# Two-layer Flamingo block on one core: logits pieces in banks of their own, gate selections behind the first pairs, first and last expert in halves of 256 rows

## What is computed

```
logits = xt @ wg                       # 2048 x 8
top two experts of each token, softmax weights of the two, renormalised
cap = 512 slots of each expert; a token's slot is its rank among those that chose the expert
y[slot] = gelu(x[slot] @ w1[e]) @ w2[e]; out[token] += gate * y[slot]
```

## Time and profile before

| | us |
|---|---|
| median of 3 runs (lowest, highest) | 574.84 (572.47, 578.08) |
| the profiled execution | 574.42 |
| its span in the trace | 572.7 |
| PE busy | 511.3 (89%) |
| DVE busy | 423.4 (74%) |
| ACT busy | 249.9 (44%) |
| POOL busy | 147.5 (26%) |

### The profile page before, as it was taken

How to read it: one execution, slowest core, us unless ns; L and a number is a source line. 1 busy time by engine, 2 the same in 40 slices (tenths; PEclk the granted TensorE clock), 3 DMA queues, 4 the chain that set the end, 5 groups by cost and what they waited for, 6 DMA issues and landing times.

```text
span 572.7 us, 8595 instructions
## 1 busy us (share of the span) xinstructions
PE 511.3 (89%) x3273; PEld 418.0 (73%) x3273; DVE 423.4 (74%) x794; ACT 249.9 (44%) x362; POOL 147.5 (26%) x120
## 2 busy tenths in 40 slices
PE   7887989897979899989999882899999999999990
PEld 3555667786969777767787651488999989999990
DVE  3799889999999885977977969564766848667340
ACT  1233566757675454526554511053534344343200
POOL 2053400000000021202212200720437355283144
PEclk9988999998989999979999995899999999999996
DMA  5511110000000010122221331211537475462031
GB/s 185 174 37 38 37 38 0 1 1 0 1 1 2 1 37 1 48 71 69 74 74 38 129 100 31 73 38 42 122 120 163 104 172 106 140 152 59 5 38 19
DMA packets 35118, 36.40 MB, mean 64 GB/s; under 512 B 3936, under 2 KB 33925, under 8 KB 34949
## 3 DMA queue, kind: packets, MB, share of 16 engines
q1 hardware_dynamic: 28933, 28.19, 15.5%
q0 software_dynamic: 6144, 7.66, 8.0%
HBM read 28.19 MB, written 8.39 MB: 64 GB/s over the span
## 4 chain that ended last, share of the span: by engine, by line
PE 58%; DVE 28%; issue 7%; ACT 3%; POOL 1%; DMA 1%; DVEq 0%; POOLq 0%; ACTq 0%
PE PS L1288 13%; PE PS L1289 13%; PE PS L1290 13%; PE PS L1619 4%; PE PS L1303 4%; PE PS L1498 3%; PE PS L1561 3%; DVE tmp L949 2%; DVE st L785 2%; DVE tmp L960 2%; PE PS L1628 2%; DVE xT_lo L809 2%; DVE hT_lo L968 2%; DVE xn L801 2%; DVE tmp L937 1%
## 5 line engine op out<-in xcount | busy, mean ns | idle before, releaser
L1288 PE MATMUL PS<-w_hi,hT_hi 128*128 128x256 f32 x384 | 110.5, 288 | 2.0 <-DVE hT_lo L968 2.0
L1290 PE MATMUL PS<-w_hi,hT_lo 128*128 128x256 f32 x384 | 109.4, 285 | 0.0
L1289 PE MATMUL PS<-w_lo,hT_hi 128*128 128x256 f32 x384 | 109.4, 285 | 0.0
L757 ACT ACTIVATE tmp<-PS,biasT 128x512 f32<-128x512 f32 x64 | 40.5, 685 | 103.9 <-PE PS L1290 103.8
L568 POOL DMA_INDIRECT out<-tmp,dst_idx x32 | 55.9, 1747 | 104.5 <-DVE tmp L1247 97.2
L1288 PE MATMUL PS<-xT_hi,w_hi 128*128 128x512 f32 (+1 forms) x200 | 79.4, 397 | 1.6 <-DVE tmp L837 1.1
L1289 PE MATMUL PS<-xT_lo,w_hi 128*128 128x512 f32 (+1 forms) x200 | 78.3, 392 | 0.0
L1290 PE MATMUL PS<-xT_hi,w_lo 128*128 128x512 f32 (+1 forms) x200 | 78.1, 391 | 0.0
L1288 PEld LDWEIGHTS PS<-w_hi,hT_hi 128*128 128x128 f32 x384 | 74.5, 194 | 3.8 <-DVE hT_lo L968 2.3
L1289 PEld LDWEIGHTS PS<-w_lo,hT_hi 128*128 128x128 f32 x384 | 74.4, 194 | 1.3
L1290 PEld LDWEIGHTS PS<-w_hi,hT_lo 128*128 128x128 f32 x384 | 74.2, 193 | 0.0
(11 more groups left out here) (211 smaller groups left out, 953.1 us busy)
## 6 DMA issues: line engine op xcount, KB each, us to landing
w_raw<-in_L_ffn_w SPq DMA_DIRECT2D x72, 256.0 KB, 3.3
residual<-in_x SPq DMA_DIRECT2D x4, 512.0 KB, 5.9
out<-residual SPq DMA_DIRECT2D x3, 512.0 KB, 4.7
normed_rows<-xn SPq DMA_DIRECT2D x3, 512.0 KB, 2.9
kv<-in_L_ffn_b SPq DMA_DIRECT2D x1, 1024.0 KB, 4.7
tmp<-in_L_xattn_Wq SPq DMA_DIRECT2D x2, 256.0 KB
out<-residual SPq DMA_DIRECT2D x2, 256.0 KB, 2.1
normed_rows<-xn SPq DMA_DIRECT2D x2, 256.0 KB, 3.1
```

Of the source, the lines that this page charges most:

```text
L757: act.activation(gD[:, G % 2, f, :], H[:, G % 2, f, :], ACT.Gelu, bias=biasT[:, col:col + 1]).then_inc(e_gelu, 1)
L1288: pe.matmul(o, lh, rh, start=start, stop=False, skip_group_check=skip)
L1289: pe.matmul(o, lh, rl, start=False, stop=False, skip_group_check=skip)
L1290: return pe.matmul(o, ll, rh, start=False, stop=stop, skip_group_check=skip)
```

## The change

1. **Piece 2** (tiles 8 to 11) is applied at t = 15 instead of 14 and turned at t = 16 instead of 15. Its logits columns and rows come after the loop instead of at t = 16, and `top_two(2)` stands after the last `x_lo`.
2. **Pieces 3 and 4** are transposed into PSUM banks of the scores (2 and 3), their logits go to banks 4 and 7. PE then waits for `c_shift`, `lgT_copied` or `lg_copied` in place of `T_free`. Before the last transpose stand 8 warming matmuls, and 5 after it (before: 3, 10 and 5). POOL's `power` of piece 3 comes before the last `low_parts` of that stage.
3. **Ranks:** three matmuls accumulate in one bank, and the DVE addition L1148 falls away. The tile-number selection goes from DVE (2 instructions) to ACT (16 small ones). The 32 instructions for `onehotB` become 4 on 1024 elements each. The small matmuls go by tile in four groups, each with a wait for ACT and one for DVE.
4. **Gate selections** are made at steps 2, 3 and 4 of the expert loop, `gates_of_slots` at step 5 (before: ahead of the loop, and at step 1), with the sums in bank 7.
5. **Experts 0 and 7** are done in two blocks of 256 rows: 40 steps instead of 32, of which 16 have `hidden` of 12 matmuls of 128x256 and `project` of 12. The first gather is of two tiles, and so is the second. Of the last expert, tiles 0 and 1 leave with the first block; tile 2 at `half_done`, and tile 3 from a bank of its own at the end.

```
-APPLY_AT, TURN_AT, COLUMNS_AT = {7: 0, 11: 1, 14: 2}, {8: 0, 12: 1, 15: 2, 16: 3}, {9: 0, 13: 1, 16: 2, 17: 3}
+APPLY_AT, TURN_AT, COLUMNS_AT = {7: 0, 11: 1, 15: 2}, {8: 0, 12: 1, 16: 2}, {9: 0, 13: 1}
+    BLOCKS = [(0, 0, 2), (0, 2, 2)] + [(e, 0, 4) for e in range(1, NE - 1)] + [(NE - 1, 0, 2), (NE - 1, 2, 2)]
+    INPUTS = [(0, 0, 2), (0, 2, 2)] + [(e, 0, 4) for e in range(1, NE)]
+    NG = len(BLOCKS) * PAIRS
+        O_last = PS[:, 1:2, 0:D]
+        def turned_bank(r):
+            if r in (NR - 2, NR - 1):
+                return PS[:, 4 + r - NR, :].rearrange("p (k n) -> p k n", k=KD)
+            return T
+        slot_sums = PS[:, 7, 0:96]
+        INPUT_AT = [None, 1] + [PAIRS * (e + 1) - 2 for e in range(1, NE)]
...
 (POOL, layer-1 attention)
+                if c == NC - 1:
+                    power(round_of(3, 3))
                 low_parts(PAIRS + 2 * c + 1)
...
 (ACT, routing)
-            act.activation(sel_tok[:, :, 0, :], onehotA, ACT.Copy, scale=part1).then_inc(rt_sel, 1)
+            act.activation(sel_tok[:, :, 0, :], onehotA, ACT.Copy, scale=part1)
+            for t in range(NT):
+                tiles = slice(t, t + NT + 1, NT)
+                ins = act.activation(sel_tok[:, tiles, 1, :], onehotA[:, tiles, :], ACT.Copy, scale=float(t))
+                if t % 4 == 3:
+                    ins.then_inc(rt_sel, 1)
...
 (DVE, end of the attention and routing)
             x_lo(r3)
             last_stats(r4)
-            link(top_two(2))
             apply(r4)
+            take_logits(2)
             take_logits(3)
             link(top_two(3))
             x_lo(r4)
+            link(top_two(2))
             take_logits(4)
...
-            link(dve.tensor_tensor(posall..., incl..., PS[:, 5, 0:256], ALU.add))
...
-                for q in range(8 * part, 8 * part + 8):
-                    ins = dve.tensor_scalar(onehotB[:, q, :], iota_b, bl[:, q:q + 1], None, ALU.is_equal)
+                here = slice(4 * part, 4 * part + 4)
+                dve.tensor_tensor(onehotB.rearrange("p (k t) n -> p k t n", k=2)[:, :, here, :],
+                                  bcast(bl.rearrange("p (k t) -> p k t", k=2)[:, :, here].unsqueeze(3), [P, 2, 4, P]),
+                                  bcast(iota_b.unsqueeze(1).unsqueeze(1), [P, 2, 4, P]), ALU.is_equal)
...
 (DVE, expert loop)
+                    if 2 <= G < 5:
+                        gate_selection(G - 2)
-                    if G == 1:
+                    if G == 6:
                         dve.wait_ge(rt_slots, 2)
...
 (PE, end of the attention)
+            logits_columns(2)
             logits_columns(3)
-            pe.wait_ge(c_shift, 2 * NT)
-            keep_warm(3, 3)
+            logits_rows(2)
             logits_rows(3)
-            keep_warm(3, 10)
+            keep_warm(5, 8)
             transpose_x(round_of(3, 4))
-            keep_warm(3, 5)
+            keep_warm(5, 5)
             logits_columns(4)
             logits_rows(4)
...
 (PE, expert loop)
             keep_warm(3, 16)
             transpose_x(NR)
-            keep_warm(3, 9)
+            keep_warm(3, 5)
-                    if G == 1:
+                    if G == 5:
                         gates_of_slots()
-                    if G == 2:
+                    if G == 7:
                         pe.wait_ge(gates_read, 1)
```

More of the change, by code:

```diff
@@ L543, in _, with gather @@
                     power(round_of(3, c - 1))
+                if c == NC - 1:
+                    power(round_of(3, 3))
                 low_parts(PAIRS + 2 * c + 1)
[L545 to L549, removed]
+            power(round_of(3, 4))
+            def gather(i):
+                if i == 0:
                     pool.wait_ge(idx_ready, 1)
@@ L571, in scatter @@
                                             compute_op=ALU.add).then_inc(added, 16)
-            gather(0)
-            gather(1)
+            for i in range(3):
+                gather(i)
             for e in range(NE):
-                if e + 2 < NE:
-                    gather(e + 2)
+                if e + 3 < len(INPUTS):
+                    gather(e + 3)
                 scatter(e)
@@ L1230, in low_parts, with expert_out @@
                                   ALU.subtract).then_inc(w_lo_ready, 1)
-            def expert_out(e):
-                if e == 0:
+            def expert_out(e, tiles, signal, count):
+                dve.wait_ge(signal, count)
+                t, w = tiles.stop - tiles.start, len(y_of)
+                if w:
+                    dve.wait_ge(y_ready, y_of[w - 1])
+                o = O_last if e == NE - 1 and tiles.start == 3 else O[:, tiles, :]
+                dve.tensor_tensor(tD[:, tiles, :], o, bcast(b2e_bc[:, e, :].unsqueeze(1), [P, t, D]),
+                                  ALU.add).then_inc(sum_ready, 1)
+                dve.wait_ge(sum_ready, w + 1)
+                for j in range(tiles.start, tiles.stop):
+                    dve.tensor_scalar(yD[:, e % 2, j, :], tD[:, j, :], slot_gate[:, 4 * e + j:4 * e + j + 1],
+                                      None, ALU.mult).then_inc(y_ready, 1)
+                y_of.append(4 * e + tiles.stop)
@@ L1234, in expert_out, with block_done @@
+            y_of = []
+            def block_done(n):
+                e, first, count = BLOCKS[n]
+                if n == 0:
                     dve.wait_ge(b2e_loaded, 16)
[L1235 to L1237 removed]
+                if e >= 2 and first == 0:
                     dve.wait_ge(added, 64 * (e - 1))
[L1240 to L1243 removed]
@@ L1266, in _ @@
-            for G in range(NE * PAIRS + LAG):
-                if G < NE * PAIRS:
-                    if G % PAIRS == 3 and G // PAIRS + 1 < NE:
-                        x_lo(NR + G // PAIRS + 1)
+                used = NB_PAIRS + PAIRS * (n + 1)
+                if n < len(BLOCKS) - 1:
+                    expert_out(e, slice(first, first + count), hT_used, used)
+                else:
+                    expert_out(e, slice(2, 3), half_done, 1)
+                    expert_out(e, slice(3, 4), hT_used, used)
```

255 lines of the change are left out of this document (131 added, 124 removed).

## The result

The changed kernel takes **564.25 us** (median of 4 runs, 563.9 to 564.67) against 573.65 us (median of 4 runs of the kernel before, 569.46 to 578.08). The ratio is 0.9846 with a 95% interval of 0.981 to 0.9883. Predicted were 567 us and a range of 563 to 572. The profiled execution took 564.4 us (span 562.7 us); against the profiled one of before that is 10.0 us less, where the sum of the prediction had 7.7.

The account below looks back on a forecast made before the run. PE bounds the dense experts; one dependency chain from the last Wo product to the first hidden product, and four serial scatters, bound the ends. Terms -7.0 + 2.1 + 0.5 - 3.3 = -7.7 gave 567 us, range 563 to 572.

Parts of the forecast that it names:

- Part 1: End of the attention: moving piece 2's logits behind the last Wo product gains 1.5 us, at most 2.6.
- Part 2: Ranks and one-hot rows: less DVE work brings the index 3.1 us earlier, part 1 included, bounds 1.2 and 4.6.
- ACT's small copy: Tile-number selection on ACT: 16 copies of 64 elements at 0.25 us each, bounds 0.17 and 0.31, making ACT the later engine.
- Part 3: First gather: with two tiles instead of four, the first hidden product starts 7.0 us earlier in all, bounds 4.5 and 8.
- Part 4: Expert 0 in halves: more hidden work, one more transposition and PE waits lose 2.1 us, bounds 1 and 4.
- the first term of part 5: Expert 7 in halves: its hidden matmuls cost another 0.5 us.
- The table load in front of the GELU of step 0: Expert 0: ACT's 1.28 us load delays the first GELU, so PE waits 0.6 us at step 2.
- The tail: After the last matmul: scatters issued earlier, the last one starting 2.9 us after it, gain 3.3 us, bounds 2.5 and 3.7.
- The chain gives less: Rival, chance 0.25: parts 1 to 3 yield less, hidden starts only 4 us earlier, 570 us.
- More gain: Rival, chance 0.08: PE finds DVE and ACT ready in expert 0 and the second tile early, 564 us.
- The halves cost what they save: Rival, chance 0.07: 256-column hidden products spaced by weight loads, up to 13 us; half of that gives 573 us.
- PE's clock in expert 0: Rival, chance 0.04: fewer warmings and PE's waits keep the clock at half through expert 0, 585 us.

Follow-up runs that it names:

- c1: The changed kernel, unedited, measured again on another occasion: 567.70 us, ratio to the kernel before 0.9887.
- e3: Changed kernel with piece 2 of the attention's logits back where it was before the change: 566.78 us, ratio to the kernel before 0.9845.
- e5: Changed kernel with POOL's power of piece 3 back behind its last subtraction: 562.04 us, ratio to the kernel before 0.9797.
- e4: Changed kernel with the tile-number selections back from ACT to DVE as 2 instructions: 565.16 us, ratio to the kernel before 0.9839.
- e11: Changed kernel with onehotB made by 32 DVE instructions again instead of 4: 563.86 us, ratio to the kernel before 0.9799.
- e1: Changed kernel with expert 0 in one block of 512 rows again: 566.26 us, ratio to the kernel before 0.9868.
- e6: Changed kernel with one more, already met, wait in front of ACT's expert loop: 564.13 us, ratio to the kernel before 0.9797.
- e9: Changed kernel with the 32 gate matmuls at step 6 of the expert loop instead of 5: 563.00 us, ratio to the kernel before 0.9815.
- e2: Changed kernel with expert 7 in one block again, its output in two parts: 570.26 us, ratio to the kernel before 0.9926.
- e8: Changed kernel without the 16 warming matmuls before the first transposition of gathered rows: 565.70 us, ratio to the kernel before 0.9865.

## Why the prediction was right, and where its terms were off

**The mechanism held.** Faster, by the two ends of the experts, and paid for in expert 0: each of the five parts has its predicted sign. The time lies 2.3 us below the sum for the profiled execution (564.4 against 566.7), 2.0 of it in the way to the first hidden product, which is 9.0 us earlier instead of 7.0. That the number is so near is in part luck: the second set of the same kernel gave 567.7 (c1), and two sets that differ by 3.4 us can't tell 564 from 567. The stretches below say more.

**Part 1** (predicted -1.5, measured -2.4 at the last transposition). The last Wo product is 2.8 us earlier instead of 2.0, of which 0.1 us lies before the first Wo product; at the transposition the gain is inside the upper bound of 2.6. The step that was too dear is the last value product, which I had at 326.4:

```profile
325.72 2.02 PE L1675 MATMUL PS<-Vblk,tmp 128*128 128x136 f32 x16
```

From it to the last Wo product it is 5.7 us, 5.8 predicted. Behind it PE has what I had counted: 6.09 us to the transposition, 6.15 predicted. e3 gives the move itself a size of 2.75 us, less 0.9 given back. The `apply` was stretched as foreseen (1.28 us against 0.72 in e5), but e5 shows that undoing this gives nothing back.

**Part 2** (with part 1 predicted -3.1, measured -4.5). Without L1148 and with the third small matmul, the way from the last transposition to `onehotA` is 0.2 us shorter (0.3 predicted). **The term that was mis-sized is ACT's small copy:** 0.25 us each in the sum, 0.15 measured (2.43 / 16), below even my lower bound of 0.17. I had drawn a line through two single ACT instructions, which puts the whole fixed time into each; a row of 16 costs less for each. The Trainium skill, "ScalarE: Activation LUTs", section "What ACT_TABLE_LOAD costs", gives such an instruction 186 ns and 0.833 ns an element, and lets neighbours overlap by 93 ns: an estimate of 0.146 us at 64 elements, with which the trace agrees (0.152). So the signal that ends the stretch is DVE's at 352.1 and not ACT's, which was to come 5.25 us after `onehotA` and would have been 352.8. e4 (+1.31) and e11 (+0.64) show the gather following DVE one for one.

**Part 3** (gather to hidden, predicted -3.9, measured -4.4). PE took the second tile 4.4 us after the first gather, the first hidden product came 1.92 us after that (1.95 predicted). I had the tile there at 4.5 us, but PE free for it only at 4.95. This half us is PE's warming: 4.88 us from the end of the last slot matmul to the first transposition instead of 5.55, with the clock back at 356 us. Without halves it is 11.1 us (e1).

**Part 4 and the first term of part 5** (predicted +2.1 and +0.5, measured +2.35 together). By the last transposition of gathered rows the 2.35 divide into 1.55 for part 4 and 0.8 for the halves of the last expert, where I had 0.5. Work: sixteen half products at 1.44 us for eight of 2.75 give +1.0, the added transposition 0.35 us (363.79 to the next hidden product at 364.14); predicted 1.0 and 0.45. Of the waits, that at step 2 isn't there. **The step that failed is the table load in front of the GELU of step 0**: that it would run after the first hidden product was taken over from the trace of before, though the change removed the very wait ahead of it; e6 puts a wait back and gets both the late load and a wait of 0.48 us at step 2. (My terms for that wait, 1.65 + 1.28 + 0.86, make 3.8 us and not 3.9, which leaves 0.5.) At the gate selections it is 0.49 us and not 1.1, and e9 removes it with one half step. The total fits nevertheless, and that is luck: some 0.6 us are spread over the experts in slips of under 0.3 us between steps, for which the trace names no releaser and I had no term. Late GELUs of ACT raise the price of part 4 from 1.55 to 3.1 us in c1 and to 3.3 in e3, inside my bounds of 1 and 4, and in e2, with the clock down, to 4.9, outside them.

**The tail** (predicted -3.3, measured -3.4). POOL's third scatter started 0.92 us after the last matmul, the fourth 2.79; predicted 1.05 and 2.9. e2 takes this part alone back: +3.36.

**The rivals.** *The chain gives less* fell with the 9.0 us. *More gain* (564) was the closest in its number, by an earlier first hidden product; ACT was ready in expert 0 and DVE 0.49 us late, but the second tile came no earlier. *The halves cost what they save* fell at 0.12 us a matmul in the half products. *PE's clock in expert 0*: the granted clock was 1.00 throughout expert 0 after, and e8, without the 16 warmings, has it back at 362 us and the same time in the experts. But it is not ruled out for every execution: in e2 the clock did fall in expert 0, once, behind a wait of PE of 2.34 us, and came back within 4 us. The Trainium skill ("TensorE: Matmul & The Clock Gate", section "HAM oscillation") warns that waits between bursts bring the clock down again and again; no profile shows the again and again. Waits of 0.48 and 0.85 us in e6 and of 2.04 us in c1 left the clock at 1.00; the fall in e2 is the one case that agrees.

## What to carry to other kernels

A wait that a change removes also frees what is queued behind it on that engine; look for table loads there before taking their place from the old trace. When work moves from one engine to another, price a run of small instructions by a run of small instructions, not by a line through single ones. And where executions differ upstream by more than the edit is worth, measure the edit between two points of the trace around it.

## What the runs showed of the hardware that was not expected

- ACT's table load is held back by a second wait in front of it even when that wait is already met: 359.98 us without it, 361.96 us with it, worth 1.0 us in all.
- Which of DVE's instructions is held until POOL's 2.4 us subtraction ends depends on the order of POOL's queue: a 0.17 us one before, the `apply` after, the residual in e5 (0.48 to 2.50 us). Not every one is held: the `x_lo` at 326.98 ran through it in its usual 1.23 us.
- The clock's dips come at different places from one execution of the same kernel to the next: 3.1 us between first and last Wo product.
- ACT's GELU started 0.6 to 2 us late in expert 0 in 3 of 13 profiles of the changed kernel and its edits (c1, e2, e3), with no cause that the traces name. Not explained.
- In one of these (e2) PE then waited 2.34 us, and the granted clock was at 0.50 from 375 to 378 us while PE worked; after a wait of 2.04 us in c1 it stayed at 1.00.
